# A Mamba-2 mixer with a post-norm LoRA layer: the group loop written out, and two VectorE steps put elsewhere

## The reference, cut to what matters

```
proj = x @ in_proj_w.T                      # gate (8192), hs (8192), B (8x128), C (8x128), dt (128)
hs, B, C = silu(conv4(hs, B, C) + conv_b)   # causal convolution with 4 taps along the sequence
dt = softplus(dt + dt_bias);  A = -exp(A_log)
# per head h (128 heads of 64 channels, 16 heads share a group's B and C), chunks of 128 tokens:
Y  = (C B^T * exp(segsum(dt A))) @ (hs dt)  # inside the chunk
Y += exp(cumsum(dt A)) * (C @ state)        # from the chunks before, "off the diagonal"
state = decay * state + B^T @ (hs dt decay)
g = (Y + hs D) * silu(gate)
out = g * rsqrt(mean over the group of g^2 + 1e-5) * norm_w @ out_proj_w.T
x = layernorm(x + out);  x = layernorm(x + x @ W.T + bias + lora(x))
```

## Time and profile before

| | |
|---|---|
| median of three runs | 1759.04 us |
| the profiled execution | 1757.22 us, span 1755.4 us |
| mean granted TensorE clock | 0.976 |
| PE busy | 1634.2 us, 93% |
| DVE busy | 1337.6 us, 76% |
| ACT busy | 1231.3 us, 70% |
| POOL busy | 1003.5 us, 57% |
| HBM | 101 GB/s over the span |

### The profile page before, as it was taken

How to read it: one execution, slowest core, us unless ns; L and a number is a source line. 1 busy time by engine, 2 the same in 40 slices (tenths; PEclk the granted TensorE clock), 3 DMA queues, 4 the chain that set the end, 5 groups by cost and what they waited for, 6 DMA issues and landing times. The chain is left out here.

```text
span 1755.4 us, 29902 instructions
## 1 busy us (share of the span) xinstructions
PE 1634.2 (93%) x9056; PEld 1301.8 (74%) x9056; DVE 1337.6 (76%) x1864; ACT 1231.3 (70%) x2383; POOL 1003.5 (57%) x815
## 2 busy tenths in 40 slices
PE   7569999999989999899989999899998999999888
PEld 5447787777867788677867878677786778777655
DVE  6458698777958689686986779686896869877676
ACT  5377866776767877588766778677776786677742
POOL 2145666656546656566565566456565565665654
PEclk9879999999989999999999999999999999999999
DMA  3644434445334433444435443344454443553411
GB/s 106 117 146 108 109 93 103 119 97 114 91 95 113 106 103 88 112 99 110 96 107 102 94 120 91 87 117 102 101 90 111 108 114 90 108 114 98 128 37 42
DMA packets 237263, 179.19 MB, mean 102 GB/s; under 512 B 17296, under 2 KB 199568, under 8 KB 236688
## 3 DMA queue, kind: packets, MB, share of 16 engines
q1 hardware_dynamic: 237072, 176.94, 41.9%
HBM read 172.17 MB, written 4.72 MB: 101 GB/s over the span
## 5 line engine op out<-in xcount | busy, mean ns | idle before, releaser
L936 POOL TENSOR_TENSOR w_lo<-raw,w_hi 128x512 fp32r<-128x512 f32 x209 | 292.4, 1399 | 408.6 <-ACT w_hi L704 406.1
L502 PE MATMUL proj<-x_hi,w_hi 128*128 128x512 f32 x1160 | 467.9, 403 | 62.1 <-POOL w_lo L936 32.4
L503 PE MATMUL proj<-x_lo,w_hi 128*128 128x512 f32 x1160 | 456.8, 394 | 0.0
L504 PE MATMUL proj<-x_hi,w_lo 128*128 128x512 f32 x1160 | 456.1, 393 | 0.0
L1074 DVE SCALAR_TENSOR_TENSOR hs<-proj,uch,hs 128x511 f32<-128x511 f32 (+2 forms) x384 | 285.4, 744 | 73.6 <-ACT hs L729 68.3
L784 ACT ACTIVATE decay<-decay,tok 128x128 f32<-128x128 f32 x1024 | 312.2, 391 | 4.2 <-DMA decay<-acum_d 4.2
L502 PEld LDWEIGHTS proj<-x_hi,w_hi 128*128 128x128 f32 x1160 | 221.1, 191 | 108.7 <-issue 60.5
L975 POOL TENSOR_TENSOR dh<-dh,eac 128x512 f32<-128x512 f32 x96 | 123.4, 1286 | 267.0 <-DVE eac L1122 267.0
L504 PEld LDWEIGHTS proj<-x_hi,w_lo 128*128 128x128 f32 x1160 | 220.7, 190 | 47.1
L503 PEld LDWEIGHTS proj<-x_lo,w_hi 128*128 128x128 f32 x1160 | 221.4, 191 | 42.0
L1096 DVE TENSOR_TENSOR decay<-decay,cb 128x1024 f32<-128x1024 f32 x128 | 182.6, 1427 | 87.8 <-ACT decay L790 85.2
(11 more groups left out here) (113 smaller groups left out, 2738.9 us busy)
## 6 DMA issues: line engine op xcount, KB each, us to landing
decay<-acum_d SPq DMA_DIRECT2D x128, 512.0 KB, 8.8
raw<-w_t SPq DMA_DIRECT2D x209, 256.0 KB, 6.2
eac<-eacum_d SPq DMA_DIRECT2D x192, 128.0 KB, 8.5
wo_raw<-wo_t SPq DMA_DIRECT2D x32, 256.0 KB, 5.9
c_new<-wo_t SPq DMA_DIRECT2D x32, 256.0 KB, 8.1
hs<-x_t SPq DMA_DIRECT2D x4, 512.0 KB, 6.4
acc<-x_tok SPq DMA_DIRECT2D x1, 2048.0 KB, 9.6
out<-acc SPq DMA_DIRECT2D x8, 256.0 KB, 2.0
```

Source lines behind the costliest of these rows:

```text
L502: nc.tensor.matmul(dst[:], w_hi[:, ws, k, :], x_hi[:, k, cols], start=(k == 0), stop=False)
L503: nc.tensor.matmul(dst[:], w_hi[:, ws, k, :], x_lo[:, k, cols], start=False, stop=False)
L504: mm = nc.tensor.matmul(dst[:], w_lo[:, ws, k, :], x_hi[:, k, cols], start=False, stop=(k == KC - 1))
L936: nc.gpsimd.tensor_tensor(w_lo[:, s].rearrange("p a b -> p (a b)"), raw[:, s, :], w_hi[:, s].rearrange("p a b -> p (a b)").bitcast(F32), A ...
```

## The change

There are three edits. First, groups(body) is a plain Python loop that emits the body for each g from 0 to 7, so g is an int everywhere, no engine has a loop instruction, and the tests for isinstance fall away. Second, take_var moves from behind the y addition to in front of it in three steps around a group change: (1,7), where it reads the variance of chunk 5, and (0,0) and (0,1), where it reads those of chunks 6 and 7 of the group before. In steps (1,2) to (1,6) it stays behind. Third, the scale_off calls that stood at the start of their step stand at the end of the step before, behind the remaining taps and in front of add_out and of the c = 0 wo_split_lo. Nothing computed changes.

```diff
-        def groups(eng, body):
-
-            body(0, False)
-            with eng.Fori(1, GROUPS - 1) as g:
-                body(g, False)
-            body(GROUPS - 1, True)
+        def groups(body):
+
+            for g in range(GROUPS):
+                body(g, g == GROUPS - 1)
...
                         s = step(g, e, c)
                         off, ne, ncn = after(e, c)
-                        if c % CPB and len(STEP_TILES[e][c - 1]) > 1:
-                            scale_off(g, e, c)
-
...
+                        if e == 1 and c == 7:
+                            take_var(g, 5)
+                        elif e == 0 and c < 2 and g > 0:
+                            take_var(g - 1, 6 + c)
+
                         dve.wait_ge(yd_ready, s + 1)
...
                         nc.vector.tensor_tensor(y[:], p_yd[:], dh[:], ALU.add).then_inc(y_ready, 1)
-                        if e == 1 and c > 1:
+                        if e == 1 and 1 < c < 7:
                             take_var(g, c - 2)
-                        elif e == 0 and c < 2 and not (isinstance(g, int) and g == 0):
-                            take_var(g - 1, 6 + c)
...
                         for t in rest:
                             conv(g, t)
+                        if c < 7 and (c + 1) % CPB and len(STEP_TILES[e][c]) > 1:
+                            scale_off(g, e, c + 1)
 
                         if e == 1 and c > 0:
                             add_out(g, c - 1)
```

More of the change, by code:

```diff
@@ L324, in free_w @@
             elif g is not None:
-                if isinstance(g, int) and g == 0:
+                if g == 0:
                     p = PROLOGUE[k]
@@ L478, in body @@
                                 sp.dma_start(dst, src).then_inc(ffn_loaded, 16)
-            groups(sp, body)
+            groups(body)
             for t in range(CHUNKS):
@@ L636, in body @@
                             project(g, todo.pop(0))
-                        if isinstance(g, int) and s == 0:
+                        if s == 0:
                             front(0, 0, 0)
@@ L641, in body @@
                             norm_sum(g, c - 2, last)
-                        elif e == 0 and c < 2 and not (isinstance(g, int) and g == 0):
+                        elif e == 0 and c < 2 and not (g == 0):
                             norm_sum(g - 1, 6 + c, False)
@@ L674, in body @@
                             project_out(g, 0, 7)
-                        elif not (isinstance(g, int) and g == 0):
+                        elif not (g == 0):
                             project_out(g - 1, 1, 7)
@@ L680, in body @@
                             lora_down(c - 3)
-            groups(pe, body)
+            groups(body)
             project_out(G, 1, 7)
@@ L780, in gaps @@
                 act.wait_ge(decay_loaded[dslot(c)], 16 * decay_round(g, e, c))
-                if c == 0 and not (isinstance(g, int) and 2 * g + e == 0):
+                if c == 0 and not (2 * g + e == 0):
                     act.wait_ge(unit_loaded[e], 48 * g + 32)
@@ L922, in body @@
                             nc.scalar.activation(half[:, pc, :], p_out[:], ACT.Copy).then_inc(half_saved, 1)
-            groups(act, body)
+            groups(body)
             for t in range(5, CHUNKS):
@@ L1013, in gate_y @@
                     gg = g if e else g - 1
-                    if isinstance(g, int) and g == 0 and e == 0:
+                    if g == 0 and e == 0:
                         gg, tiles = None, [t for t in PROLOGUE if t.kind == "G0"]
@@ L1042, in add_bias @@
                 nc.gpsimd.tensor_tensor(acc[:, t, :], acc[:, t, :], bias_sb, ALU.add).then_inc(biased, 1)
-            groups(pool, body)
+            groups(body)
             inv_rms(G, 6)
@@ L1268, in body @@
                             tap(g, tiles[0], 1, 3)
-                        if isinstance(g, int) and g == 0 and (e, c) == (1, 2):
+                        if g == 0 and (e, c) == (1, 2):
                             dve.wait_ge(acc_loaded, 16)
@@ L1307, in body @@
                             conv(g, t)
+                        if c < 7 and (c + 1) % CPB and len(STEP_TILES[e][c]) > 1:
+                            scale_off(g, e, c + 1)
                         if e == 1 and c > 0:
                             add_out(g, c - 1)
-                        elif e == 0 and c == 0 and not (isinstance(g, int) and g == 0):
+                        elif e == 0 and c == 0 and not (g == 0):
                             add_out(g - 1, 7)
@@ L1318, in body @@
                             add_ffn(c - 4)
-            groups(dve, body)
+            groups(body)
             add_normed(G, 6)
```

## The result

The changed kernel takes 1708.84 us (median of four, 1704.13 to 1709.12) against 1759.24 for the kernel before: a ratio of 0.971, interval 0.968 to 0.9741. That is 50 us less, where 69 were forecast, and 4 us above the range. The profiled execution has a span of 1706.9 us, 48.5 less than before.

The account below looks back on a forecast made before the run. TensorE, busy 93%, was taken as the bound, losing time to loop jumps and to waits for the variance read and scaling. Savings 41.5 + 16.0 + 8.5 + 3.0 = 69.0 us from 1757.2 gave 1688 us, range 1679 to 1705.

Parts of the forecast that it names:

- Part 1: Group changes: writing out the loop removes five taken jumps costing 42.05 us; term 41.5 us, bounds 39.5 to 42.5.
- The clock's part should go with the stall: Group changes after a jump: half-level clock, 3.6 us in the 20.80 us stretch checked, disappears once the jump's stall does.
- Part 2: Steps (1,7), (0,0), (0,1): variance read ahead of y removes L525's fourteen waits; 16 us, bounds 11 and 16.2.
- the wait vanishes: Step (1,7): with the read earlier, L525 starts when the transposes are issued, about 494.6 instead of 496.44.
- I take 16: Gain taken for all fourteen variance waits: seven of about 1.7 us and seven shorter in (0,1), together 16.2 us.
- Part 3: Scaling moved ahead of the trailing sum at seven places a group: 8.5 us from L655's waits, 3.0 from L549's.
- The second rival: Jump stalls go, but PE waits anew on p_hid, w_lo and wo_lo: 1716 us, halfway 1702; chance 0.12.

Follow-up runs that it names:

- e1: Kernel before with only its loop written out, variance read and scaling not moved: 1722.67 us, 0.9771 of the kernel before.
- e9: Kernel before with two groups written out in each loop pass, two taken jumps instead of five: 1732.03 us, 0.9849 of the kernel before.
- e10: Changed kernel with the variance read put back behind the y addition, on e11's chip: 1699.73 us, 0.9661 of the kernel before.
- e11: Changed kernel unaltered, on e10's chip: 1705.12 us, 0.9694 of the kernel before.
- e2: Changed kernel with the variance read put back behind the y addition, on the chip of e1 and e3: 1705.49 us, 0.9679 of the kernel before.
- e6: Changed kernel with the decay load ahead of the weight tile cut to an eighth, so the result is incomplete: 1689.6 us, 0.9607 of the kernel before.
- e7: Changed kernel with the w_hi and w_lo splits in (0,0) put behind work not needing the late tile: 1694.16 us, 0.9635 of the kernel before.
- e8: Changed kernel with the weight tile issued ahead of the decay and eac loads in (1,7): 1703.75 us, 0.9687 of the kernel before.
- e12: e7 with the variance read put back behind the y addition: 1696.04 us, 0.9655 of the kernel before.
- e3: Changed kernel with the scaling put back at the start of its own step: 1719.22 us, 0.9758 of the kernel before.
- e5: Changed kernel unaltered, on e6's chip: 1704.51 us, 0.9695 of the kernel before.

## Why the prediction was wrong

Part 1 was right in kind and nearly in size. Its term was 41.5 us; e1 measures 40, e9 26 for three jumps, and the changes are at 10.2 us and a clock of 1.00. No new stall came with the new code. But one of its steps, "The clock's part should go with the stall", was too simple. In three of the five changes with a jump the clock was at its half level for 3.4 us already ahead of the stall, right behind the variance wait of 1.7 us (the earlier trace rows is such a place):

```profile
497.10:500.50 3.40, 3.40 (x9) 2.65 (x8) 2.79 (x4) 1.44 (x3) 3.40 (x4) 0.50 0.21 65
```

The others start at 910.1 and 1323.1. Such a stretch costs 1.5 us in e1, so some 4.5 of the 42.05 us, by estimate, were not the jumps'. e1 still has two of them. That the term came so close is in part luck.

Part 2 is the step that failed: "the wait vanishes" and "I take 16". The wait in (1,7) did vanish. But I asked what is late next only for the one instruction, L525, and answered with the transposes beside it. The first y of the next group comes 1.3 us earlier after the p_yd products of (1,7) (12.1 us for the 13.4 of e1; with the read behind y, in e10, it is 12.8), and there ScalarE's w_hi depends on a load whose issue hangs on w_lo of the step before and whose flight takes some 10 us beside the decay load. It does not come earlier with PE. The seven short waits in (0,1), 4.3 of the 16 us, hang on that chain as well; they grew to 1.2 to 1.5 us each. The measured worth is -5 us (e10 against e11) instead of +16. The term was also counted on waits that part 3 shortens by itself, from 1.8 us (e1) to 1.2 (e2), so that only 10.8 us of them were left to win.

Part 3, taken alone, was right about p_st and too low in all: forecast at 11.5 us, it brings 17.2 (e1 against e2). p_st's waits go in full. Beyond that it shortens the variance waits by 6.5 us, and the two slow-clock stretches of e1, 3 us, are absent. L547's waits, forecast to fall by 3, do not fall (3.9 us in e1, 6.4 in e2, 4.4 in e10). In the changed kernel edit 2 spoils part of that: p_st waits 4.6 us in (0,1), and L547's waits are 8.3, as they end one VectorE chain later than the late mix. With part 1 alone as the base, the two edits together bring 0.9771 - 0.971 to 0.9771 - 0.9695, some 11 to 13 us against 27.5.

The second rival, "the waits of PE come back under other names" (1702 halfway, 1716 in full), is what happened, at 1709. I gave it 0.12 because I looked for room on VectorE and POOL by their busy shares, which is no evidence on a DMA's landing. The evidence lay in the trace of before: five of the seven changes were hidden by the stall that the change removes, and of the two that were not, I read the length only. With the landing out of the way the sum nearly comes out: e6, without that part of the work, takes 1689.6 us where 1688 was forecast.

## What to carry to other kernels

A stall that is taken away was cover for everything else that was in flight. Read what follows it at a place where it does not occur, engine by engine, loads included, before the other savings are added to it. When a load is late, see what is queued behind its consumer in the same instruction stream: putting that first (e7) gained more than reordering the loads (e8), which only exchanged one late landing for another. And where two edits work on one chain, measure each alone: here one brought 17 us, and the other took 5 of them back.

## What the runs showed of the hardware

PE's wait of 1.7 to 1.8 us in (1,7), with small matmuls on both sides, was followed within 1 us by 3.4 us at a granted clock of 0.50 in three of seven changes of the kernel before, two of seven of e1 and two of seven of e9. In e1 such a change takes 12.40 instead of 10.90 us. The same wait was not followed by it in the other changes, nor were the 1.2 us waits there in e2, e10 and e12 (21 changes), nor p_st's waits of up to 3.2 us in (0,1) of e3, where the clock stayed at 1.00. What decides this is open.

A taken jump costs PE some 8 to 9 us in this kernel (8.0 in e1, 8.8 in e9); its branch record at L300 lasts 9.6 us in the median, those of the other engines 0.04 to 0.06. The Trainium skill ("Runtime: NRT & Kernel Launch", section "Instruction fetch mechanics") says that a taken branch breaks the sequential prefetch. e1 and e9 agree in that PE stalls where the loop jumps and not where it runs on; that it is the fetch which PE waits for, no run here shows. The 108 ns of the "Control Flow Timing" section of the Trainium skill's "Advanced Engine Details and Errata" do not describe what PE pays here.

Measured from the start of the p_yd products of (1,7), the tile lands after 14.2 us in the mean of seven changes with the read in front of y (e11) and after 13.0 with it behind (e10). The traces of the changed kernel, e5 and e7 have 14.1, 13.7 and 14.0, those of e2 and e12 13.1 and 13.3. With the read in front, the loads of the next step are issued 0.7 us sooner (10.4 for 11.1 us) and could share the queues with the tile, but that was not tried. From its issue the tile takes 7.6 to 11.2 us behind the full decay load (e5), 5.6 to 7.2 behind an eighth of it (e6), and 2.7 to 4.3 when it is issued ahead of it (e8).
